# Attention scores of a decoder layer: two heads issued together every second slot, or one head in every slot

## The reference

```
x = x + attn_fourier(layernorm(x))      # FFTs, cumulative sum, inverse FFT
x = x + xattn(layernorm(x), ctx, ctx)   # 16 heads of 64, causal mask and ALiBi
x = x + ffn(layernorm(x))               # two top-2-of-64 layers of Kronecker experts
# xattn, for each head:
logits  = q @ k.T / sqrt(64) + causal + slope * (i - j)
weights = softmax(logits)
attn    = weights @ v
# then: concat(attn) @ Wo + bo
```

## Time and profile before

| | |
|---|---|
| median of 3 executions | 2180.39 us |
| lowest and highest | 2177.41 and 2185.89 us |
| the profiled execution's own time | 2180.39 us |
| its span, first to last instruction | 2178.5 us |
| mean granted TensorE clock | 0.927 |
| busy: PE, DVE, ACT, POOL | 1947.4, 1283.8, 1252.4, 277.6 us |

### The profile page before, as it was taken

One profiled execution on the slowest core, in us unless ns is written; L12 is line 12 of the kernel. 1 busy time (PEld: TensorE's weight loads), 2 busy tenths in 40 slices (PEclk: granted clock), 3 DMA queues, 4 the chain that ended last, 5 costly groups with the idle time before them and its releaser, 6 DMA issues.

```text
span 2178.5 us, 47368 instructions
## 1 busy us (share of the span) xinstructions
PE 1947.4 (89%) x13298; PEld 1458.5 (67%) x13298; DVE 1283.8 (59%) x5457; ACT 1252.4 (57%) x4007; POOL 277.6 (13%) x593
## 2 busy tenths in 40 slices
PE   7998988989898989988989889888989999899975
PEld 5767667675766757667676676767767577675754
DVE  1456555666565666656565556665656656566664
ACT  2475564757556485564755547565474755648553
POOL 3020200203021030200202002020110302102010
PEclk9998999999999898989989899898998989989887
DMA  7000000000000000000000000000000000000000
GB/s 226 1 11 1 7 11 8 11 2 16 2 7 11 7 11 1 7 11 8 11 2 7 11 8 11 2 16 2 7 11 2 16 2 7 11 7 2 1 6 6
DMA packets 18600, 27.65 MB, mean 13 GB/s; under 512 B 2178, under 2 KB 17027, under 8 KB 17923
## 3 DMA queue, kind: packets, MB, share of 16 engines
q1 hardware_dynamic: 18274, 23.84, 3.4%
HBM read 19.65 MB, written 4.19 MB: 11 GB/s over the span
## 4 chain that ended last, share of the span: by engine, by line
PE 63%; DVE 14%; issue 12%; ACT 4%; DVEq 3%; POOL 2%; ACTq 1%; POOLq 0%
PE G L788 7%; PE O L732 5%; PE G L759 5%; PE PT L690 4%; PE G L815 4%; PE S L719 3%; PE S L717 3%; PE S L632 3%; DVE chosen_dn L275 2%; PE S L642 2%; DVE yT L1042 2%; DVE shared L908 2%; PE FA L801 2%; PE PT L672 2%; ACT chosen_up L262 1%
## 5 line engine op out<-in xcount | busy, mean ns | idle before, releaser
L508 ACT ACTIVATE shared<-shared,neg_max 128x128 f32<-128x128 f32 (+1 forms) x512 | 204.9, 447 | 297.8 <-DVE neg_max L908 296.4
L262 ACT COPY chosen_up<-experts 32x128 f32 x1024 | 251.6, 291 | 44.9 <-issue 38.5
L788 PE MATMUL G<-chosen_up,W 128*64 128x256 f32 x1024 | 260.5, 394 | 8.0 <-DVE pre L1032 8.0
L908 DVE CUSTOM_DVE_ANT_0 shared<-S,neg_bias 128x128 f32<-128x128 f32 (+1 forms) x512 | 162.4, 355 | 127.7 <-PE S L719 122.1
L690 PE MATMUL PT<-ident,shared 128*128 128x128 f32 x768 | 161.0, 326 | 77.9 <-DVE shared L901 65.1
L275 ACT COPY chosen_dn<-experts 64x64 f32 x1024 | 197.7, 240 | 52.9 <-issue 36.5
L275 DVE COPY chosen_dn<-experts 64x64 f32 x1024 | 152.4, 189 | 67.6 <-issue 57.5
L262 DVE COPY chosen_up<-experts 32x128 f32 x768 | 171.9, 255 | 32.3 <-issue 27.1
L388 POOL TENSOR_SCALAR var_eps<-moments 128x2 f32<-128x2 f32 x48 | 10.4, 217 | 1355.7 <-DVE moments L845 1345.5
L1032 DVE SCALAR_TENSOR_TENSOR pre<-G,scale_up,bias_up 64x256 f32<-64x256 f32 x256 | 123.2, 481 | 87.5 <-PE G L788 79.8
L815 PE MATMUL G<-chosen_dn,W 128*32 128x64 f32 x2048 | 157.5, 237 | 18.5 <-DVE W L1019 18.5
(11 more groups left out here) (164 smaller groups left out, 3819.4 us busy)
## 6 DMA issues: line engine op xcount, KB each, us to landing
x<-in_x SPq DMA_DIRECT2D x16, 256.0 KB, 2.7
ctxT<-in_ctxT SPq DMA_DIRECT2D x16, 256.0 KB, 2.9
out<-xn SPq DMA_DIRECT2D x16, 256.0 KB, 3.1
neg_bias<-in_neg_bias SPq DMA_DIRECT2D x1, 2048.0 KB, 13.3
wk<-in_xWk SPq DMA_DIRECT2D x1, 1024.0 KB
wo<-in_xWo SPq DMA_DIRECT2D x1, 1024.0 KB
wv<-in_xWv SPq DMA_DIRECT2D x1, 1024.0 KB, 7.7
wq<-in_xWq SPq DMA_DIRECT2D x1, 1024.0 KB, 9.7
```

The costliest lines, as they stand in the source:

```text
L262: last = copy(dst, src.rearrange("p (m c) -> p m c", m=2))
L508: act.activation(probs[i % 3][:, lo:hi], probs[i % 3][:, lo:hi], ACT.Exp, bias=neg_max[:, i % 3, rt:rt + 1], scale=-1.0).then_inc(probs_re ...
L788: mm = pe.matmul(G[g % 2 * F1:(g % 2 + 1) * F1, 0:n], up_W(g)[:, k * F1:(k + 1) * F1], chosen_up[g % UP_SLOTS][:, k * n:(k + 1) * n], star ...
L908: dve.tensor_tensor_reduce(probs[i % 3][:, lo:hi], S[i % 2][:, lo:hi], neg_bias[:, i, (1 - rt) * P:2 * P], 1.0, TOP, ALU.add, ALU.min, neg ...
```

## The change

`score_pair` is gone. The scores of one head are issued in its own slot, for i from 0 to 15, between the transposes of head i-2 and the value products of head i-3. The number of matmuls, their shapes, operands and banks are the same. The wait for `scores_masked` is dropped: bank S[i%2] was last read by the mask of head i-2, and the transposes of head i-2 in the same slot have already waited for its exponentials, which come after that mask. The wait for the query and key projections stays at every fourth head. VectorE's and ScalarE's programs are untouched; their semaphore counts are the same.

```
-                if i < HEADS and i % 2 == 0:
-                    score_pair(b, i)
+                if i < HEADS:
+                    m, lo = i // 2, (i % 2) * KEY
+                    if i % 4 == 0:
+                        pe.wait_ge(proj_kept, at(b, 26, 20 + i // 2))
+                    pe.matmul(S[i % 2][:, 0:P], qT[lo:lo + KEY, m, 0:P], kT[lo:lo + KEY, m, 0:P], start=True, stop=True)
+                    pe.matmul(S[i % 2][:, P:3 * P], qT[lo:lo + KEY, m, P:2 * P], kT[lo:lo + KEY, m, :],
+                              start=True, stop=True).then_inc(scores_done, 1)
...
-            def score_pair(b, i):
-
-                m, halves = i // 2, (slice(0, KEY), slice(KEY, P))
-                if i % 4 == 0:
-                    pe.wait_ge(proj_kept, at(b, 26, 20 + i // 2))
-                if i > 0:
-                    pe.wait_ge(scores_masked, at(b, 32, 2 * i))
-                for s, rows in zip(S, halves):
-                    pe.matmul(s[:, 0:P], qT[rows, m, 0:P], kT[rows, m, 0:P], start=True, stop=True)
-                for s, rows in zip(S, halves):
-                    pe.matmul(s[:, P:3 * P], qT[rows, m, P:2 * P], kT[rows, m, :],
-                              start=True, stop=True).then_inc(scores_done, 1)
```

## The result

The changed kernel takes 2298.18 us (median of 4, 2265.78 to 2302.68), the kernel before 2178.9 us on the same chip. The ratio is 1.0474, 95% interval 1.0395 to 1.0556: slower by 4.7%, inside the forecast range and above the forecast 2265 us.

What follows compares the result with a forecast made beforehand. TensorE, busy 1947.4 of 2178.5 us, was taken as the bound: +5.08 us times 15 joined passes = 76, batch 0 +8, clock 0, so 2180.4 + 84 = 2265 us, +3.9%; range 2212 to 2345.

Steps and rivals of the forecast that it cites:

- 84 and 0: Whole kernel: 84 us of added TensorE time (76 in 15 joined passes, 8 in batch 0), net 0 from the clock.
- A single head costs 0.85 us, with 0.10 for the switch from transposes: Scores in an odd slot: 0.85 plus 0.10 after transposes plus 0.10 before value products, 1.05 us in all.
- Rival 1: Odd heads' scores: a 64-row product alone takes half the time, an odd head adds 0.63 us, 2224 us in all; 10%.
- The estimate of 0.66 us: Single head's scores, from the skill page's four-tile figure: 0.66 us, an odd head adds 0.86, time 2246 us.
- Two heads at full clock take 6.14 us: Head slots beside the FFN: two heads at full clock take about 6.1 us, against 5.36 before.
- The gaps shrink to 1.5 and 0.93: TensorE's idle gaps after head 3's slot began and in slot 12: from 2.47 and 1.88 to these us.
- Head 1: +0.95 us: Head 1's scores, ahead of the second query projection, push later work back by 0.85 + 0.10 us per joined pass.
- Heads 5, 7, 9, 11, 13, 15 and the tail: 1.05, 1.05, 0.78, -0.12, 1.05, 0.92, -0.6: Us per joined pass: full price at 5, 7, 13; less reserve at 9, 15; head 11 in a gap; tail waits shrink.
- Batch 0: +8 us: Batch 0's attention, without FFN beside it: no TensorE reserve, 8 odd heads at about 1.0 us each.
- The clock: first stretch 3 to 7 us longer, second gone, net 0 (-21 to +6 us): Half-clock stretches in head slots: longer first costs +1.7 to +3.4 us per pass, avoided second saves about 3.0.
- Rival 2: Head slots after the first gap: clock stays down, first stretch longer than 20 us, +8.5 us per pass, 2393 us; 13%.

Runs made afterwards that it cites:

- twin_fill: Changed kernel plus unused 128-row products in TensorE's gaps (slots 4, 12) and, from head 4, each score product repeated on the other 64 rows: 2148.43 us, ratio 0.9836.
- before_fill: Kernel before plus unused 128-row products in TensorE's two idle gaps, four in slot 4 and three in slot 12: 2087.92 us, ratio 0.9562.
- after_fill: Changed kernel plus unused 128-row products in TensorE's gaps, two in slot 4 and one in slot 12: 2225.61 us, ratio 1.011.

## Why the prediction was right, and where it wasn't

The direction and the mechanism of TensorE's part held: a head alone costs what a pair cost. The sum had the wrong shape inside, and that the total came so near is partly luck, since two errors of opposite sign stood in it. In ratios, TensorE's time is twin_fill minus before_fill, 0.9836 - 0.9562 = 2.7%, 60 us; the clock is the rest, (1.0474 - 0.9836) - (1 - 0.9562) = 2.0%, 44 us; by the intervals of the four ratios this second part is known to about 20 us. I had 84 and 0.

- *A single head costs 0.85 us, with 0.10 for the switch from transposes*: 0.85 and 0.48 against 0.38. Right. Rival 1 (half the time) is out. The estimate of 0.66 us from the four-tile figure of the Trainium skill, page "TensorE: Matmul & The Clock Gate", Part 3, is out too: two tiles of 64 rows side by side here give the full factor of two. Four tiles of 32 rows were not run.
- *Two heads at full clock take 6.14 us*: 6.13. Right. *The gaps shrink to 1.5 and 0.93*: 1.55 and 0.84. Right.
- *Head 1: +0.95 us*. This step failed: it was +0.23 (the first window, which also holds head 3). I had assumed that it stands alone. The timeline of the kernel after shows it beside the routing's own 64-row product, which uses the other half:

```profile
1144.85 0.48 PE L757 MATMUL G<-route_diag,ones 64*128 64x256 f32 x1
1144.86 0.48 PE L696 MATMUL S<-kT,qT 64*128 64x128 f32 x2
```

From the routing's product to the second query projection it is 0.85 us now and was 0.62.

- *Heads 5, 7, 9, 11, 13, 15 and the tail: 1.05, 1.05, 0.78, -0.12, 1.05, 0.92, -0.6*: 1.13, 0.93, 0.76, -0.11, 0.78, 0.80, -0.66. Right within 0.12 us but for head 13, whose window in the earlier trace rows was at half clock and had no reserve; at full clock it has the 0.27 us of head 9's.
- *Batch 0: +8 us*. Its slots took 33.7 us and take 38.8, +5.1. Two heads went from 3.49 to 4.21 us, +0.72 instead of 1.05. I took TensorE's 3.46 busy of 3.49 us as "no reserve"; but busy time counts the pipelined ends, and from the pair's turn to the next transposes it was 0.42 us before and is 0.23 now, and from the transposes to the scores 0.55 before and 0.42 now. A third of a microsecond of waiting (0.19 + 0.13) stood inside "busy".
- *The clock: first stretch 3 to 7 us longer, second gone, net 0 (-21 to +6 us)*. The signs held, the size didn't. The second is gone in all 15 joined passes. The first lasts 17 us in seven, 27 in seven and 37 in one, so 3 to 24 us longer than in the same pass before. Rival 2, with its mark at 20 us, took place in eight of the 15, and since passes of one execution differ by up to 20 us in it, the wider scatter of whole executions (1.6%) probably comes from there. After five passes the next stage also has 3.4 us at half clock, after three of them twice (it is 74.5 us long otherwise, 76.8 after pass 8); before, after two. The net is +44 us, the mis-sized term.

## What to carry to other kernels

Here products on 64 rows came in pairs for free where nothing for all rows stood between them; taking one of a pair elsewhere cost its full price, unless it met another product on the other half there. Before weighing microseconds of order, look at the granted clock: here the half-clock stretches that began behind two gaps of 2 us cost 94 us, and 1.4 to 1.8 us of products on 128 rows in each gap took all of it back (0.9 us in each took 87), more than any reordering here. "Busy nearly all the time" is no proof that TensorE has no reserve; the distance from start to start, against the same step without a wait, is.

## What the runs showed of the hardware

- Each half of the rows keeps its own order: with the order even 128, even 256, odd 128, odd 256 columns, both 128-column products began, within 0.02 us of each other, before either 256-column one, and the time was that of the alternating order (ratio 0.9999).
- The clock went with how many rows the work used, not only with whether TensorE worked. The same added products, on 128 rows or on 64, gave 2095 or 2158 us; unused twins on the other half took the changed kernel from a ratio of 1.0474 to 1.0263. At half clock TensorE was busy without a break for 34 us (after_fill) and 37 us (after) and the clock did not rise.
- What decides that a pass gets 17, 27 or 37 us was not settled. In the trace of the kernel after, the stretches of 17 us began 9.5 to 10.2 us into the head slots, those of 27 us at 10.3 to 10.8, that of 37 us at 11.2; but no run here varied their start by itself.
